# A graph attention kernel: SyncE broadcasts lanes for two chunks at once and fetches more units row by row

## What is computed

```python
n_in, n_out = x[src], x[dst]
wn_out = n_out @ W_lin + b_lin
e_ij = leaky_relu(concat([n_in, n_out]) @ W_att + b_att)     # slope 0.2
a_ij = (e_ij @ w_alpha)[:, 0]
alpha = softmax of a_ij over the edges of each receiver
n_i = segment_sum(alpha[:, None] * wn_out, src)
out = layernorm(x + elu(n_i))
```

## Time and profile before

| | |
|---|---|
| median of three runs | 2303.85 us (2301.32 to 2305.96) |
| the profiled execution | span 2302.9 us, 0.95 us under that median; what lies around its span is not shown |
| granted TensorE clock, mean | 0.947 |
| gathers on POOL | 1,635 |
| single rows by SP | 3,200, by 400 loads of eight addresses |
| lane broadcasts by SP | 415 of 128 KB |

### The profile page before, as it was taken

One profiled execution on the slowest core, in us unless ns is written; L12 is line 12 of the kernel. 1 busy time (PEld: TensorE's weight loads), 2 busy tenths in 40 slices (PEclk: granted clock), 3 DMA queues, 4 the chain that ended last, 5 costly groups with the idle time before them and its releaser, 6 DMA issues.

```text
span 2302.9 us, 62793 instructions
## 1 busy us (share of the span) xinstructions
PE 1790.7 (78%) x11498; PEld 1460.1 (63%) x11705; DVE 1753.5 (76%) x5214; ACT 1463.3 (64%) x4913; POOL 1626.4 (71%) x1670
## 2 busy tenths in 40 slices
PE   4658788877878888887878787878888788787770
PEld 2337676766667666766666666666666666666660
DVE  9849887877789787786888787878766666666667
ACT  2327687876667666665666666666666666666665
POOL 2067777777777777777777777777777777777760
PEclk9769999999999999998999999999899999999995
DMA  3145555555455555554555555555555555555541
GB/s 120 60 113 136 133 136 131 132 128 140 127 134 131 134 132 133 132 136 127 131 131 130 127 136 134 132 131 129 132 138 135 135 134 135 133 135 134 132 111 56
DMA packets 165719, 294.14 MB, mean 128 GB/s; under 512 B 40002, under 2 KB 110014, under 8 KB 165329
## 3 DMA queue, kind: packets, MB, share of 16 engines
q0 software_dynamic: 78864, 216.03, 36.8%
q1 hardware_dynamic: 85733, 73.82, 13.0%
q10 hardware_dynamic: 732, 0.27, 0.1%
HBM read 278.95 MB, written 11.02 MB: 126 GB/s over the span
## 4 chain that ended last, share of the span: by engine, by line
POOL 22%; issue 12%; PE 10%; DMA 7%; DVE 3%; DVEq 1%; ACT 0%; POOLq 0%; ACTq 0%
POOL rows L650 22%; DMA rows<-qv_table,senders 7%; PE masked_ps L977 3%; PE hidden_ps L966 2%; PE turned_ps L992 2%; PE hidden_ps L964 2%; PE turned_ps L984 1%; DVE sums L1579 1%; DVE spare L1670 0%; DVE leaky L1535 0%; PE masked_ps L976 0%; DVEq L1579 0%; DVE x_sb L1665 0%; ACT x_sb L853 0%; DVE sums L1655 0%
## 5 line engine op out<-in xcount | busy, mean ns | idle before, releaser
L650 POOL DMA_INDIRECT rows<-qv_table,senders x1635 | 1598.4, 978 | 498.3 <-issue 465.7
L964 PE MATMUL hidden_ps<-identf,rows 128*128 128x128 f32 x1635 | 466.4, 285 | 311.4 <-DMA rows<-qv_table,senders 298.6
L1579 DVE SCALAR_TENSOR_TENSOR sums<-sums,shrink,turned_ps 128x129 f32 x1660 | 571.2, 344 | 81.3 <-issue 26.9
L992 PEld LDWEIGHTS turned_ps<-rows,spare 128*128 128x128 f32 x3270 | 439.0, 192 | 299.8 <-ACT spare L777 212.4
L762 ACT ACTIVATE spare<-masked_ps,peaks 128x128 f32<-128x128 f32 x1660 | 472.8, 368 | 218.6 <-DVE peaks L1557 216.9
L966 PE MATMUL hidden_ps<-onehotT,p_unit 128*128 128x128 f32 x3320 | 602.4, 284 | 0.0
L1542 DVE TENSOR_REDUCE lows<-masked_ps 128x4 f32<-128x512 f32 x415 | 285.8, 689 | 401.2 <-PE masked_ps L977 399.6
L966 PEld LDWEIGHTS hidden_ps<-onehotT,p_unit 128*128 128x128 f32 x3320 | 531.7, 201 | 0.9 <-issue 0.9
L992 PE MATMUL turned_ps<-rows,spare 128*128 128x129 f32 x3270 | 473.0, 279 | 60.8 <-DVE sums L1579 54.6
L752 ACT ACTIVATE sloped<-hidden_ps 128x512 f32<-128x512 f32 x415 | 249.2, 600 | 345.7 <-PE hidden_ps L966 342.6
L964 PEld LDWEIGHTS hidden_ps<-identf,rows 128*128 128x128 f32 x1635 | 239.2, 146 | 356.2 <-issue 332.1
(11 more groups left out here) (201 smaller groups left out, 865.6 us busy)
## 6 DMA issues: line engine op xcount, KB each, us to landing
lanes_all<-lane_list SPq DMA_DIRECT2D x415, 128.0 KB
single_rows<-qv_table SPq DMA_DIRECT2D x3200, 1.0 KB
rows<-qv_table,senders POOLq DMA_INDIRECT x1635
qv_table<-rows SPq DMA_DIRECT2D x24, 257.0 KB, 2.7
out<-x_sb SPq DMA_DIRECT2D x1, 1344.0 KB
out<-x_sb SPq DMA_DIRECT2D x1, 896.0 KB
kept<-windows SPq DMA_DIRECT2D x3, 208.0 KB
out<-x_sb SPq DMA_DIRECT2D x1, 448.0 KB
```

The source lines that it names most:

```text
L650: g.indirect_dma_start(out=rows[:, k % U, c, :], out_offset=None, in_=table, in_offset=bass.IndirectOffsetOnAxis(ap=senders[:, s % 2, c * ...
L964: t.matmul(whole[:, unit], rows_at_unit(k, c)[:, 0:F], identf[:], is_transpose=True, start=True, stop=False, skip_group_check=True)
L992: mm = t.matmul(unit_sums_ps[:, c, :], weights[:, k % 2, c * P:(c + 1) * P], rows_at_unit(k, c)[:, F:R], start=True, stop=True)
L1579: v.scalar_tensor_tensor(out=at, in0=at, scalar=shrink[:, k % 4, i:i + 1], in1=unit_sums_ps[:, i, :], op0=ALU.mult, op1=ALU.add).then_inc( ...
```

## The change

SP's loop goes over pairs of chunks. `lanes_of` broadcasts the 2 KB of two chunks by one DMA of 256 KB into two neighbouring places of `lanes_all`; the ring still holds four chunks, and has two semaphores. It waits for the one-hot of chunk k - 3 (that of k - 4 was made before it). `besides` of both chunks follows, and then `fetch_rows`, once for a pair. A single unit is now due every 12th chunk (k = 11, 23, ..., 407: 34 units), and its 128 rows are split over six passes of 21 or 22 rows, whose addresses come by one load each. `make_onehot` waits for the semaphore of the pair. `gather` is not edited, but `units_by_pool` follows from `ROW_CHUNKS`, so three gathers are issued at these 34 chunks.

```diff
--- before.py
+++ after.py
@@ -101,8 +101,9 @@
     LANE_RING = 4
 
 
-    ROWS_EACH = 8
-    ROW_CHUNKS = -(-UNIT // ROWS_EACH)
+    ROW_PAIRS = 6
+    ROW_CHUNKS = 2 * ROW_PAIRS
+    ROWS_TO = [UNIT * n // ROW_PAIRS for n in range(ROW_PAIRS + 1)]
     RING_S = 2
     COUNTS_S = 4
     def run_ends_of(s):
@@ -366,7 +367,7 @@
         lanes_made = sem("lanes_made")
         lanes_ready = sem("lanes_ready")
         lanes_stored = [sem(f"lanes_stored{s}") for s in range(SETS)]
-        lanes_in = [sem(f"lanes_in{r}") for r in range(LANE_RING)]
+        lanes_in = [sem(f"lanes_in{r}") for r in range(LANE_RING // 2)]
         unpacked = sem("unpacked")
         blocks_ready = sem("blocks_ready")
         cleared = sem("cleared")
@@ -507,14 +508,16 @@
             store_lanes(0)
 
             def lanes_of(k):
+
                 s, n = place(k)
+                m = min(2, NCH - k)
                 if k >= LANE_RING:
-                    sp.wait_ge(onehotT_ready, k - LANE_RING + 1)
+                    sp.wait_ge(onehotT_ready, k - LANE_RING + m)
                 if n == 0:
                     sp.wait_ge(lanes_stored[s], 16)
-                sp.dma_start(lanes_all[:, k % LANE_RING, :],
-                             lanes_dram[s][n * CHUNK:(n + 1) * CHUNK].rearrange("(a e) -> a e", a=1).to_broadcast([P, CHUNK])
-                             ).then_inc(lanes_in[k % LANE_RING], 16)
+                sp.dma_start(lanes_all[:, k % LANE_RING:k % LANE_RING + m, :].rearrange("p m e -> p (m e)"),
+                             lanes_dram[s][n * CHUNK:(n + m) * CHUNK].rearrange("(a e) -> a e", a=1).to_broadcast([P, m * CHUNK])
+                             ).then_inc(lanes_in[k // 2 % (LANE_RING // 2)], 16)
 
             def besides(k):
                 if k == RAW_AT:
@@ -554,27 +557,27 @@
                 if n not in single_of:
                     return
                 s, row = place(single_of[n])
-                first = k % ROW_CHUNKS * ROWS_EACH
+                first, end = ROWS_TO[k % ROW_CHUNKS // 2], ROWS_TO[k % ROW_CHUNKS // 2 + 1]
                 if first == 0:
                     sp.wait_ge(single_ready, s + 1)
                     if n >= RING_S:
                         sp.wait_ge(high_sums_done, single_of[n - RING_S] + 1)
-                for r in range(first, min(first + ROWS_EACH, UNIT), 8):
-                    starts = nc.values_load_multi_w_load_instructions(
-                        single_at[row:row + 1, s % 2, r:r + 8], engines=(mybir.EngineType.SP,), min_val=0,
-                        max_val=(PAD_ROW + P - 1) * R,
-                        skip_runtime_bounds_check_because="they are rows of the table, times the length of a row")[1]
-                    for i in range(8):
-                        sp.dma_start(single_rows[r + i:r + i + 1, n % RING_S, :],
-                                     flat_table[bass.ds(starts[i], R)].rearrange("(a r) -> a r", a=1)
-                                     ).then_inc(fetched_in(n)[0], 16)
+                starts = nc.values_load_multi_w_load_instructions(
+                    single_at[row:row + 1, s % 2, first:end], engines=(mybir.EngineType.SP,), min_val=0,
+                    max_val=(PAD_ROW + P - 1) * R,
+                    skip_runtime_bounds_check_because="they are rows of the table, times the length of a row")[1]
+                for r in range(first, end):
+                    sp.dma_start(single_rows[r:r + 1, n % RING_S, :],
+                                 flat_table[bass.ds(starts[r - first], R)].rearrange("(a r) -> a r", a=1)
+                                 ).then_inc(fetched_in(n)[0], 16)
 
             sp.wait_ge(qv_stored[0], 16 * (PAIRS - PAIRS // 2))
             sp.wait_ge(qv_stored[1], 16 * (PAIRS // 2))
             sp.wait_ge(pad_rows_stored, 16)
-            for k in range(NCH):
+            for k in range(0, NCH, 2):
                 lanes_of(k)
                 besides(k)
+                besides(k + 1)
                 fetch_rows(k)
 
             for first, end in BATCHES:
@@ -1523,7 +1526,7 @@
 
 
             def make_onehot(k):
-                dve.wait_ge(lanes_in[k % LANE_RING], (k // LANE_RING + 1) * 16)
+                dve.wait_ge(lanes_in[k // 2 % (LANE_RING // 2)], (k // LANE_RING + 1) * 16)
                 if k >= 4:
                     dve.wait_ge(masked_done, k - 3)
                 v.tensor_scalar(onehotT[:, k % 4, :], lanes_all[:, k % LANE_RING, :], part_f[:], None, ALU.is_equal).then_inc(onehotT_ready, 1)
```

## The result

The changed kernel takes 2864.43 us (median of five runs, 2863.53 to 2867.3), the kernel before 2305.96 us beside it (five runs, 2301.32 to 2308.22). The ratio is 1.243, with a 95% interval from 1.241 to 1.244: slower by 24%, where 2434 us was forecast and 2299 to 2508 given as the range.

What follows compares the result with a forecast made beforehand. POOL's gathers bound the kernel, with SP close behind; SP becomes the limit. First broadcast at 139.2 us, 204 passes x 10.66, 19 of other transfers, 2.7 landing, 97.45 tail and 0.95 to the median give 2434 us; range 2299 to 2508.

Steps and rivals of the forecast that it cites:

- What bounds the kernel, and what stands behind it: POOL's gathers are the limit at 5.08 us a chunk; SP's loop is close behind at 4.48 us, 88%.
- Fewer gathers: POOL issues 1,626 gathers, nine fewer: 11.6 us off, which counts only while POOL is the limit.
- A pass of SP, 9.81 us plus D: SP's loop for two chunks: 9.81 us plus the larger address load's extra cost, 10.66 us in all.
- 2260.5 + 204 D: Whole time in us with SP the limit; 204 passes each pay the larger address load's extra cost over one of eight.
- The unknown D: SP's load of 21 or 22 addresses costs 0.85 us more than one of eight, 1.58 us; bounds nothing to 1.21.
- ACT as a stand-in: ACT's load of one number, 0.278 us, taken for SP's, so seven more addresses cost 0.448 us, 64 ns each.
- The broadcast, the ring and what is moved past: On SP: doubled broadcast issues in the same time, coarser ring waits cost nothing, other transfers stay at 19 us.
- The load is nearly a fixed price: Rival: SP's address load grows under 0.16 us, POOL stays the limit, 2292 us; chance 0.15.
- The floor of about 600 ns: Skill's figure for SP's address load: 16 ns an address beyond it, 0.21 us extra, about 2303 us.
- Even: Rival: SP's address load costs 0.19 to 0.23 us more, time 2299 to 2308 us; chance 0.06.
- Between: Rival: SP's load has a larger fixed part than ACT's, 0.23 to 0.6 us more, 2308 to 2383; chance 0.11.
- The load doesn't go out as one: Rival: SP's 21 addresses go as loads of 8, 8 and 5, 2.01 us, time 2522 us; chance 0.08.

Runs made afterwards that it cites:

- The pairs alone: The changed kernel with a unit every 16 chunks as before, in 8 passes of 16 rows: 2305.56 us against 2303.10, ratio 1.0005.
- the runs with a unit every 14 chunks: The changed kernel with 7 passes of 16 or 24 rows: 2301.66 us, ratio 1.0004; repeated 2300.82, ratio 1.0000; with LANE_RING 8 in place of 4, 2300.67, ratio 0.9999.
- the first, second and fifth run above: The changed kernel with loads begun at multiples of 8 (2486.32 us), at multiples of 4 (2473.68 us), and with rows split at multiples of 4 (2426.01 us).
- loads of 4, 2, 1 and 1: The kernel before, with its load of eight addresses replaced by four loads of 4, 2, 1 and 1: 2431.12 us, one run.
- every 12, unpaired: The kernel before with a unit every 12 chunks, chunks not paired, 8 or 12 rows in a pass: 2575.33 us, ratio 1.119.
- counts of four: The changed kernel with its rows split at multiples of 4, so loads of 20 and 24 numbers: 2426.01 us, ratio 1.054.
- starts at a multiple of 4: The changed kernel with each load begun at the multiple of 4 at or below its first row: 2473.68 us, one run.
- starts at a multiple of 8: The changed kernel with each load begun at the multiple of 8 at or below its first row: 2486.32 us, ratio 1.079.
- before, shifted: The kernel before with its addresses written one number (4 bytes) further on in their tile: 2548.51 us, one run.

## Why the prediction was right or wrong, by its steps

**What bounds the kernel, and what stands behind it: right.** POOL was the limit and SP the next, with a tenth to spare. The pairs alone left the time as it was, and each kernel that gave SP more than 10.1 us for two chunks was slower.

**Fewer gathers: right in number, and hidden as forecast; their worth was not confirmed.** 1,626 gathers were issued, and POOL waited for PE. That nine fewer would give 11.6 us where POOL is the limit is not borne out by the runs with a unit every 14 chunks: four fewer should have given 5.2 us there, and no gain could be measured.

**A pass of SP, 9.81 us plus D: right.** 21 rows took 8.13 us, (8.13 - 0.23) / 20 = 0.395 us apart, where 0.39 stood in the sum. The mean of the six loads' medians is 3.68 us, so D was 3.68 - 0.726 = 2.96, and the prediction's own 2260.5 + 204 D gives 2864 us, where 2864.43 was measured. So close a hit is partly luck. SP's loop, from the first broadcast at 137.8 us to the last row, whose issue ends at 2769.0, took 2631 us, where 204 x 12.77 + 19 = 2624 stand in the sum with this D. What follows came out shorter by as much; the row that answers to the earlier trace rows, PE's first product of chunk 407:

```profile
2770.70 0.45 PE L967 MATMUL hidden_ps<-identf,rows 128*128 128x128 f32 x1 [4.75 <-DMA single_rows<-qv_table]
```

It started 1.7 us after the last row's issue (2.7 in the sum), and from it to the end of the span are 91.6 us (97.45 in the sum). For the loads of the first, second and fifth run above, with means of 1.80, 1.72 and 1.49 us, 2260.5 + 204 D gives 2479, 2464 and 2417; measured were 2486, 2474 and 2426. So the sum holds to about 10 us, and nearly all of the error lies in D.

**The unknown D: wrong, and it is the step that failed.** "13.33 x 0.064 = 0.85 us, a load of 1.58 us" stood for all six loads. For the two that begin at a multiple of 64 it was near, 1.63 and 1.66 us, though in part by luck (next step). For the four others it was short by three. "From above: in proportion, 13.33 x 0.726 / 8 = 1.21 us" was no upper bound: it takes for granted that a longer load is at worst as dear by the number as the one shown, 0.091 us, and the ill-placed ones here cost 0.22 (4.60 / 21). Every load of several numbers in the trace of before began at a multiple of 8, so the rows could not show the other price. The diff did: 128 rows over six passes begin at 21, 42, 85 and 106, and this was not looked at as something that might have a price. The fall of the time outside the range is this one term: 204 x (2.96 - 0.85) = 430 us.

**ACT as a stand-in: right for one number, and not the reason for 0.064.** SP's loads of one number take what ACT's take. But what lies between one and eight is not seven equal steps, so it is luck that 0.064 comes near the 0.058 us a number (0.232 / 4) of a well-placed load. The runs give, for a start at a multiple of 4 numbers, about 0.26 us, 0.232 for each four, and 0.207 for each one left over; for the other starts tried, 0.26 us and 0.207 for every number (the medians of each start are over all its loads):

| numbers | start | median us, where | by these prices |
|---|---|---|---|
| 4 | multiple of 8 | 0.50, loads of 4, 2, 1 and 1 | 0.49 |
| 8 | multiple of 8 | 0.73, before | 0.72 |
| 12 | multiple of 4 | 0.96, every 12, unpaired | 0.96 |
| 16 | multiple of 8 | 1.19, pairs alone | 1.19 |
| 20 | multiple of 4 | 1.42, counts of four | 1.42 |
| 21 | multiple of 64 | 1.63 and 1.66, the change | 1.63 |
| 22 | multiple of 4 | 1.85, starts at a multiple of 4 | 1.83 |
| 24 | multiple of 8 | 1.66, starts at a multiple of 8 | 1.65 |
| 26 | multiple of 8 | 2.08, the same | 2.07 |
| 8 | 1 beyond | 1.91, before, shifted | 1.92 |
| 21 | 21 and 85 | 4.60, the change | 4.61 |
| 22 | 42 and 106 | 4.81 and 4.80, the change | 4.81 |

**The broadcast, the ring and what is moved past: right.** The issue took 0.358 us as before. A broadcast landed 3.5 us after its issue, where the store taken for comparison took 2.7; the 2.7 in the sum stands for the last rows, not for a broadcast. The waits of 25.1 and 13.0 us at the side transfers went, as forecast (1.8 us is left at what was line 536).

**The rivals.** "The load is nearly a fixed price" is refuted: loads took from 0.27 to 4.8 us. The floor of about 600 ns in the Trainium skill ("DMA: Bandwidth & Descriptors", Latency and other measured facts) does not hold here: SP's loads of one number took 0.27 to 0.28 us. "Even" and "Between" fall with D at 2.96 us. "The load doesn't go out as one" had the right side of the forecast, but not the reason: 204 loads stand in the trace, one for each pass. (By its own figures its load of five would take 0.214 + 5 x 0.064 = 0.53 us and not 0.56, which makes 2517 us of 2522.) No rival had the cause: none gave a price to where a load begins.

## What to carry to other kernels

Before a load of several numbers into SP's registers is resized, work out where each one begins. In these runs a load that began at a multiple of four 32-bit numbers was paid by fours, with a little more for each number left over; the others were paid number by number, some three times dearer at 21. Other engines' loads of several numbers were not tried. A price taken from rows holds for what those rows have in common, their placement too; an upper bound "in proportion" does not cover a property that none of the rows varied. And when a line's median is far from its minimum, look at its instructions one by one, in the order in which the loop makes them.

## What the runs showed of the hardware that was not expected

SP's register load has two prices, by whether its first number lies at a multiple of four numbers (16 bytes) in its tile: 0.726 us for eight on it, 1.91 us one number beyond, with nothing else changed. The other starts that were tried with eight numbers or more lie one or two beyond such a multiple. A load does not catch up on the way: one of 21 that begins at 21 costs 4.60 us, though after three numbers it has come to a multiple of four. Loads of one and two numbers are cheaper than the longer ones' prices say, 0.28 and 0.50 us, at the starts that were tried (two at a multiple of four, one at two and three beyond it).
